# A gated cross-attention and quantised feed-forward layer on one core: VectorE's 128x4 passes take two tensors, batch 1 is loaded later, GpSimd quantises the last 128 tokens of each batch, and the orders of all engines are listed anew

## What is computed

```python
x = x + tanh(g_xattn) * attention(layernorm(x), ctx)          # 16 heads, 64 keys, biases on q, k, v, o
h = bit_linear(layernorm(x), w1)                              # 256 -> 1024
h = silu(depthwise_conv1d(h, conv_w) + conv_b)                # 3 taps along the 512 tokens
x = x + tanh(g_ffn) * bit_linear(h, w2)                       # 1024 -> 256
# bit_linear: act_quant rounds every token to 8 bits by its own largest |value|,
#   scale = 127 / clip(max|x|, 1e-5); weight_quant makes w -1, 0 or +1 by the mean |w|
```

## Time and profile before

| | |
|---|---|
| median of 3 runs | 168.42 us (167.06 to 169.79) |
| the profiled execution's own time | 169.36 us |
| its span, first to last instruction | 167.2 us |
| PE busy | 143.8 us (86%) |
| VectorE busy | 135.2 us (81%) |
| ScalarE busy | 112.3 us (67%) |
| GpSimd busy | 88.3 us (53%) |
| mean granted TensorE clock | 0.98 of full speed |

### The profile page before, as it was taken

One profiled execution on the slowest core, in us unless ns is written; L12 is line 12 of the kernel. 1 busy time (PEld: TensorE's weight loads), 2 busy tenths in 40 slices (PEclk: granted clock), 3 DMA queues, 4 the chain that ended last, 5 costly groups with the idle time before them and its releaser, 6 DMA issues.

```text
span 167.2 us, 3548 instructions
## 1 busy us (share of the span) xinstructions
PE 143.8 (86%) x1314; PEld 79.1 (47%) x1324; DVE 135.2 (81%) x240; ACT 112.3 (67%) x176; POOL 88.3 (53%) x88
## 2 busy tenths in 40 slices
PE   7839979999799999999999796999565999984792
PEld 3238435424565336652576242568333353743461
DVE  6455999961953669995837999999999969989993
ACT  0304598779616488899999997999498586652220
POOL 0204899999910542398370089882979943200330
PEclk9996999999999999999999999999998799999999
DMA  4999800000000000000000000000030000110024
GB/s 134 269 386 395 339 6 0 4 0 0 0 0 2 4 0 0 0 0 4 4 2 0 4 0 2 0 6 0 0 125 0 4 4 0 67 67 0 3 79 169
DMA packets 5919, 8.68 MB, mean 52 GB/s; under 512 B 528, under 2 KB 4880, under 8 KB 5648
## 3 DMA queue, kind: packets, MB, share of 16 engines
q1 hardware_dynamic: 4608, 5.51, 9.6%
q10 hardware_dynamic: 1296, 2.97, 4.7%
HBM read 6.38 MB, written 2.10 MB: 51 GB/s over the span
## 4 chain that ended last, share of the span: by engine, by line
PE 29%; DVE 24%; ACT 24%; issue 15%; DMA 5%; ACTq 1%; DVEq 0%
ACT hid L1181 6%; DMA w_attn<-attn_w 5%; PE ps L445 5%; DVE u L790 4%; DVE mx L720 4%; ACT probs L1120 3%; PE ps L311 3%; DVE hid_q L860 3%; DVE hmax L812 3%; PE ps L348 3%; PE ps L507 2%; ACT side L1169 2%; ACT xn L1079 2%; PE ps L397 2%; DVE top L768 2%
## 5 line engine op out<-in xcount | busy, mean ns | idle before, releaser
L790 DVE TENSOR_TENSOR u<-ps,deq_b 128x512 f32<-128x512 f32 x32 | 20.2, 679 | 4.1 <-PE ps L436 3.6
L1433 POOL TENSOR_TENSOR hid<-hid,side 128x512 f32<-128x512 f32 x12 | 15.6, 1305 | 8.8 <-ACT side L1166 8.8
L720 DVE TENSOR_REDUCE mx<-ps 128x16 f32<-128x1024 f32 x16 | 18.8, 1212 | 1.4 <-PE ps L321 1.4
L445 PE MATMUL ps<-u,conv_w 32*32 32x512 f32 (+1 forms) x576 | 18.5, 544 | 0.9 <-ACT hid L1188 0.7
L1120 ACT ACTIVATE probs<-ps 128x1024 f32<-128x1024 f32 x16 | 15.4, 1029 | 5.6 <-PE ps L348 5.5
L1445 POOL TENSOR_TENSOR x_s<-x_s,grown 128x512 f32<-128x512 f32 x6 | 7.6, 1277 | 21.1 <-ACT grown L1198 21.1
L860 DVE TENSOR_TENSOR hid_q<-hid,ps 128x1024 f16<-128x1024 f32 x16 | 18.6, 1215 | 0.0
L436 PE MATMUL ps<-xqT,w1q 128*128 128x512 bf16 x57 | 15.3, 397 | 3.6 <-ACT xqT L1139 2.9
L1440 POOL TENSOR_TENSOR hid<-hid,side 128x512 f32<-128x512 f32 x12 | 15.5, 1305 | 4.2 <-ACT side L1169 3.8
L507 PE MATMUL ps<-w2q,hid_q 128*128 128x256 f16 x128 | 15.6, 273 | 1.3 <-DVE hid_q L860 1.3
L311 PE MATMUL ps<-xT,w_attn 128*128 128x512 f32 x32 | 15.0, 601 | 0.9 <-DVE mx L720 0.9
(11 more groups left out here) (125 smaller groups left out, 307.2 us busy)
## 6 DMA issues: line engine op xcount, KB each, us to landing
x_s<-x SPq DMA_DIRECT2D x4, 512.0 KB, 12.2
out<-x_s SPq DMA_DIRECT2D x6, 256.0 KB, 2.1
hid<-w_t SPq DMA_DIRECT2D x1, 1024.0 KB, 18.4
hid<-w_t ACTq DMA_DIRECT2D x1, 1024.0 KB, 12.3
w_attn<-attn_w ACTq DMA_DIRECT2D x1, 512.0 KB, 10.0
out<-x_s SPq DMA_DIRECT2D x4, 128.0 KB, 1.8
conv_w<-conv_d ACTq DMA_DIRECT2D x1, 384.0 KB, 13.1
w_attn<-attn_w SPq DMA_DIRECT2D x1, 256.0 KB, 5.7
```

Of the source, the lines that this page charges most:

```text
L445: last = nc.tensor.matmul(ps[ROWS * g:ROWS * g + ROWS, banks[s], first:first + n], conv_w[rg, 4 * q + s, tap, :], u[rg, 4 * q + s, first + ...
L720: nc.vector.tensor_reduce(mx[:, b % 2, k, 0:HEADS], ps[:, bank:bank + 2, :].rearrange("p c (h k) -> p (c h) k", k=KEYS), AX.X, ALU.max).th ...
L790: nc.vector.tensor_tensor(u[:, f, 1:N + 1], ps[:, bank, :], deq1_b[:, b % 2, :], ALU.mult).then_inc(u_ready.sem, 1)
L1433: nc.gpsimd.tensor_tensor(dst, dst, side[:, m % TMPS, 0, :], ALU.add).then_inc(left_ready.sem, 1)
```

## The change

Five things are edited.

1. VectorE's small passes over one value for each token (128x4, or 128x2 for batch 3's halves) were TENSOR_SCALAR with constants. They become TENSOR_TENSOR or SCALAR_TENSOR_TENSOR, whose second operand is a constant kept in SBUF and repeated over the four columns. The pass that negates the mean is left out where ScalarE doesn't need it: of 8 such passes 3 stay (batch 1 of the first norm, batches 0 and 1 of the second). The norms subtract the mean instead.
2. SP waits for the k weights before it issues x of batches 1, 2, 3 and the second layer's weights.
3. The last tile of 128 tokens of each batch (k = 3) is quantised by GpSimd. GpSimd can't read the scale from PSUM there, so PE puts this block's scale in the next bank, ScalarE copies it to SBUF (`take_scale2`, 128x128, four times), and GpSimd multiplies.
4. VectorE sets four more constants at the start.
5. The lists of PE, VectorE, ScalarE and GpSimd are written anew, in other orders and with other PSUM banks.

```diff
+TURNED = frozenset([0, 1, 2, 3])
...
             sp.dma_start(w_attn[:, 0], attn_w[:, 0]).then_inc(wq_in, 16)
+            sp.wait_ge(wk_in, 16)
             sp.dma_start(x_s[:, 1], x_v[1]).then_inc(x_ins[1], 16)
...
-                nc.vector.tensor_scalar(var[:, b], mv[:, b, :, 1], LN_EPS, None, ALU.add).then_inc(var_ready.sem, 1)
-                nc.vector.tensor_scalar(minus_mean[:, b], mv[:, b, :, 0], -1.0, None,
-                                        ALU.mult).then_inc(var_ready.sem, 1)
+                nc.vector.tensor_tensor(var[:, b], mv[:, b, :, 1], eps[:].to_broadcast([P, T]),
+                                        ALU.add).then_inc(var_ready.sem, 1)
+                if b in SCALED:
+                    nc.vector.tensor_tensor(minus_mean[:, b], mv[:, b, :, 0], minus_one[:].to_broadcast([P, T]),
+                                            ALU.mult).then_inc(mean_ready.sem, 1)
...
-                nc.vector.tensor_scalar(step1[:, a], top1[:, a], CLIP, 1.0 / QMAX, ALU.max,
-                                        ALU.mult).then_inc(step1_ready.sem, 1)
+                nc.vector.scalar_tensor_tensor(out=step1[:, a], in0=top1[:, a], scalar=CLIP,
+                                               in1=step_of[:, 0:1].to_broadcast([P, T]), op0=ALU.max,
+                                               op1=ALU.mult).then_inc(step1_ready.sem, 1)
...
-                nc.vector.tensor_scalar(deq1[:, a], step1[:, a], wmean[:, 0:1], None,
+                nc.vector.tensor_tensor(deq1[:, a], step1[:, a], wmean[:, 0:1].to_broadcast([P, T]),
                                         ALU.mult).then_inc(scale1_ready.sem, 1)
...
+            def take_scale2(b, bank):
+                act.wait_ge(*(scale2_half_ps(0, 1) if b == SPLIT else scale2_ps(b)))
+                n = nth(b, TURNED)
+                if n:
+                    act.wait_ge(*hq_turned(n - 1))
+                nc.scalar.copy(scale2_col, ps[:, bank, (T - 1) * P:T * P]).then_inc(col_ready.sem, 1)
...
+            def quantise_hidden(b, k):
+                pool.wait_ge(*col_ready(nth(b, TURNED)))
+                if b:
+                    pool.wait_ge(*f2_ps(b - 1, k // 2))
+                tile = slice(k * P, (k + 1) * P)
+                nc.gpsimd.tensor_tensor(
+                    hid_q[:, :, tile].rearrange("p (q i) n -> p q i n", i=2),
+                    hid[:, b % 2, 0:FP, tile, :].rearrange("p q n i -> p q i n"),
+                    scale2_col.unsqueeze(1).unsqueeze(1).to_broadcast([P, FP, 2, P]),
+                    ALU.mult).then_inc(hq_turned.sem, 1)
...
             residual2(1, 0)
             residual2(1, 1)
+            quantise_hidden(2, 3)
             residual2(2, 0)
             residual2(2, 1)
+            quantise_hidden(3, 3)
```

More of the change, by code:

```diff
@@ L477, in spread_scale2_half @@
                 for k in (2 * a, 2 * a + 1):
-                    last = nc.tensor.transpose(ps[:, bank, k * P:(k + 1) * P],
+                    at = bank + (b in TURNED and k == T - 1)
+                    last = nc.tensor.transpose(ps[:, at, k * P:(k + 1) * P],
                                                qscale2[:, b % 2, k:k + 1].to_broadcast([P, P]), idf[:])
@@ new lines, in _ @@
+            hidden(0, 3, 7, p_ready(2, 0))
+            hidden(0, 4, 2, p_ready(2, 1))
+            hidden(0, 5, 3, p_ready(2, 1))
+            hidden(0, 6, 6, u_ready(0, 2))
+            hidden(0, 7, 7, u_ready(0, 3))
+            scores(3, 2, 4, p_ready(2, 2))
+            denominators(2, 0, 2, u_ready(0, 4))
+            values(2, 0, 3, u_ready(0, 5))
+            denominators(2, 1, 2)
+            values(2, 1, 0, p_ready(2, 3))
+            scores(3, 3, 6, u_ready(0, 7))
+            turn_den(2, 1, p_ready(2, 3))
@@ new lines, in _ @@
+            scores_t(3, 0, 6, deq1_ready(1), neg_ready(3))
+            scores_t(3, 1, 2, hid_ready(0, 3))
+            hidden(1, 2, 1, x1_ready(2, 0))
+            hidden(1, 3, 0, u_ready(1, 1))
+            scores_t(3, 2, 4, u_ready(1, 0), x1_ready(2, 1))
+            scores_t(3, 3, 6, p_ready(3, 0))
+            denominators(3, 0, 2, p_ready(3, 1))
+            values(3, 0, 3, p_ready(3, 1))
+            denominators(3, 1, 2)
+            values(3, 1, 1, u_ready(1, 2))
+            turn_hmax(0, 0, u_ready(1, 3))
@@ new lines, in _ @@
+            project_o(3, 0, 1, oT_ready(3, 0))
+            project_o(3, 1, 0, oT_ready(3, 1))
+            hidden(2, 0, 2, xqT_ready(2))
+            second(0, 0, 1, x1_ready(3, 0))
+            hidden(2, 1, 0, x1_ready(3, 1))
+            hidden(2, 2, 4, hid_taken(0, 2))
+            hidden(2, 3, 5, hid_ready(1, 0))
+            hidden(2, 4, 3, hid_ready(1, 1))
+            hidden(2, 5, 2, u_ready(2, 0))
+            hidden(2, 6, 0, u_ready(2, 1))
+            hidden(2, 7, 4, u_ready(2, 2))
+            second(0, 1, 5, u_ready(2, 3))
@@ new lines, in _ @@
+            convolve(2, 0, (0, 4, 6, 7), u_ready(2, 7), hid_ready(1, 3))
+            spread_deq1(3, 1, z_ready(0, 0))
+            turn_xq(3, 5, z_ready(0, 1))
+            hidden(3, 0, 5, xqT_ready(3))
+            turn_hmax(1, 3, u_ready(2, 4))
+            hidden(3, 1, 2, u_ready(2, 5))
+            hidden(3, 2, 0, hid_ready(2, 0))
+            hidden(3, 3, 1, deq1_ready(3))
+            hidden(3, 4, 5, u_ready(3, 0))
+            hidden(3, 5, 4, hid_ready(2, 1))
+            hidden(3, 6, 6, hid_ready(2, 2))
@@ L671, in _ @@
+            second(2, 0, 7, col_ready(2))
+            second(2, 1, 6, hid_taken(2, 2))
+            turn_hmax_half(3, 0, 7, z_ready(0, 4))
+            turn_hmax_half(3, 1, 4, hid_half(0, 2))
+            spread_scale2_half(3, 0, 5, hid_half(0, 3))
+            spread_scale2_half(3, 1, 2, hid_half(0, 6))
+            second(3, 0, 3, col_ready(3))
+            second(3, 1, 2, hid_taken(3, 2))
         @block.vector
```

681 lines of the change are left out of this document (324 added, 357 removed).

## The result

The changed kernel takes 176.92 us (median; 174.19 to 178.27) against 168.47 (167.06 to 169.79) for the kernel before on the same chip. The ratio is 1.042, with a 95% interval from 1.025 to 1.059: slower by 8.5 us by the medians, where 163.6 us was forecast and 159.2 to 168.0 given as the range.

A forecast was written before the change was run, and what follows sets the result against it. No engine bounds it throughout, but VectorE does from 97 to 156 us; terms -4.6 tiles, -0.4 passes left out, -1.0 start, +0.4 waits, +0.5 taps, +0.3 copies make -4.8: 163.6 us against 168.42, range 159.2 to 168.

The forecast's parts named there:

- the five passes: VectorE's mean-negating passes left out: worth between 0 and 0.85 us, taken as -0.4 us.
- The start: Loads up to the first row maximum: k weights at 8.5 us, first maximum near 22.7; -1.0 us, bounds -3.4 and +2.
- the start gives it back: Rival: x of batch 3 lands 2 us later, so the start's -1.0 becomes +2.0; 166.6 us, chance 0.17.
- The small passes: VectorE's 22 passes on six lines, 10.4 us with 6.7 of waits for GpSimd; waits taken to grow, +0.4 us.
- waits stay: The forecast's own case: small VectorE passes still wait for GpSimd; 163.6 us, range 161.5 to 166, chance 0.43.
- The tiles: Four quantiser tiles moved to GpSimd at 2.6 us each: -4.6 us on VectorE, +0.5 for taps, +0.3 for copies.
- a slow tile: Rival: GpSimd's tile takes longer than 2.6 us, delaying `second` on PE; 172.4 us at 5.2 per tile, chance 0.10.
- The lists: New instruction orders: 0 us, bounds -2 and +2, as VectorE idles only 3.2 us between 97 and 156 us.
- The clock: PE at half clock from 13 to 15 us; a shorter gap before it may save about 1 us.
- the tile and the end: Signs: GpSimd's tile at 2.4 to 2.6 us; VectorE's last three tiles in 3.5 us, GpSimd's done before them.
- The small lines: Sign on L702, L779, L794, L801, L854, L859: mean near 0.17 us says waits gone, 0.3 to 0.9 says they stay.
- The sign for the loads: The prediction would be wrong if x of batches 1 to 3 landed later than 19.5 us.

The follow-up runs named there:

- e13: Changed kernel with SP's wait out and scale2's small passes in PSUM, GpSimd's norms still subtracting: 170.97 us, ratio 1.015 to the kernel before.
- e4: Kernel before with only GpSimd's norms changed, to subtract the mean: 178.50 us, ratio 1.057.
- e12: Changed kernel with GpSimd's norms adding and scale2's small passes in PSUM, SP's wait kept where the change has it: 167.47 us, ratio 0.987 to the kernel before.
- e11: Kernel before with only SP's wait for the k weights added, ahead of x of batches 1 to 3: 169.47 us, ratio 1.008.
- e6: Changed kernel with GpSimd's norms adding, SP's wait out and scale2's small passes in PSUM: 162.79 us, ratio 0.960 to the kernel before.
- e3: Changed kernel with GpSimd's norms adding the negated mean and SP's wait out: 168.79 us, ratio 0.984 to the kernel before.
- e7: Changed kernel with norms adding, SP's wait out and all 16 last-layer quantiser tiles on VectorE: 171.53 us, ratio 1.005 to the kernel before.
- e8: Kernel before with GpSimd's norms reading the mean from `mv` but still adding it: 169.32 us in one execution.
- e14: e3 run again for a second trace: 168.69 us in one execution.
- e1: Changed kernel with only GpSimd's norms put back to adding the negated mean: 173.37 us, ratio 1.025 to the kernel before.
- e5: Changed kernel with norms adding, SP's wait out and VectorE's small passes in the old TENSOR_SCALAR form: 167.54 us, ratio 0.988 to the kernel before.

## Why the prediction was wrong

- **The step that failed first** is one that has no term in the sum. The description of the change says "The norms subtract the mean instead"; the prediction counts the five passes that this leaves out at 0.4 us and takes the norms themselves as unchanged. They cost GpSimd 13.4 us, more than its four tiles (9.7), and 8.2 to 9.4 us of time (e13, e4). No row of before could give the price of a subtraction on GpSimd; but an operation without a row wanted two bounds, as the two-tensor passes got, and none was written.
- **The start** was forecast as a gain of 1.0. The k weights landed near 9.06 us (8.5 forecast) and PE's first matmul on them came at 9.19: right. The rule for the rest looked only at the *last* load, x of batch 3. The one that decides is x of batch 1, because VectorE's list has its statistics ahead of the values and of everything else; it landed at 16.4 us. The prediction names what is queued behind the held SP, but of batch 1 it follows only ScalarE's norm, not VectorE's list. The rival "the start gives it back" had the right place, the first row maxima, and nearly their delay (2 us; 26.13 is 2.8 later), but it names the wrong load (VectorE comes to the statistics of batches 2 and 3 at 22.42 us and doesn't wait for them), and it has no idle PE and no clock in it. Measured, the wait costs +4.7 us in the new lists (e12) and +1.4 in the old (e11).
- **The small passes** were put down as "waits stay", and that is half of what happened. In single passes L702 took 2.20 us, L801 1.04, L859 1.12, L870 0.91, held by GpSimd to its end each time. But the 22 passes of the six lines took 7.7 us where they took 10.4; at 0.13 to 0.16 us for one that isn't held, some 4.4 us of that are waits, against 6.7 before: a third of the waits went, and the sum had them grow by 0.4. The Trainium skill (SBUF — State Buffer, "Who interferes with whom") says that a VectorE instruction with two SBUF inputs contends with a GpSimd instruction that reads SBUF; the trace agrees, with 2.20 us for 0.16 of work. Its other half, that a VectorE instruction with at most one SBUF input and outside the two-port modes doesn't contend with GpSimd, agrees with e6's 0.17 us. How long such a pass waits isn't GpSimd's busy share, by which the prediction scaled it: beside the same run of additions it was 4.85 us in e3 and 1.09 in e7.
- **The tiles** were right in their durations: GpSimd's took 2.43 us (2.6 forecast; 2.37 to 5.2 given), ScalarE's copy 0.27 (0.3), VectorE's last three 3.48 (3.45). The rival of a slow tile didn't occur. Of their worth in time, 3.4 us in the sum (4.6 less 0.5, 0.3 and 0.4), no run shows it alone: e7's 2.7 to 3.5 us are near it, with a difference in the waits beside them.
- **The lists** were taken at 0 with bounds of 2 us. e3 and e6 differ by 4.0 to 6.0 us, in e3's trace most of it through one wait in one place of the new order, so these bounds were too narrow: an order's worth isn't limited by the idle time in VectorE's row, since a held pass counts as busy. In the changed kernel this wait was short (0.24 and 1.12 us), so it is no part of the miss.
- **The clock** was read only at 13 to 15 us. Each of the large losses came with a second one there: a gap on PE, and then work at 1.2 GHz or near it (6.44 us for 3.67 us of q projection, 5.11 for 3.40 of convolution).

Of the listed signs, the tile and the end held. The small lines gave no single answer: means of 0.67 (L702), 0.46 (L859) and 0.36 us (L801) told "stay", 0.16 (L794), 0.19 (L854) and 0.23 (L779) told "gone" or nearly so. The sign for the loads, x of batches 1 to 3 later than 19.5 us, would have passed the load that did the harm (16.4 us), and there was no sign for the norms. With the two faults out and the waits of `scale2` taken away, the kernel comes to 162.8 us, 0.8 below the forecast; that is not the forecast's case, which had the waits in it. Put into the prediction's own sum, the two failed steps give the miss to within 0.6 us: 163.6 + 8.2 (subtraction, e13) + 5.7 (start, +4.7 by e12 for -1.0) = 177.5 us, and 176.92 was measured. The other terms can still be off against one another.

## What to carry to other kernels

Price every line that a diff rewrites, also one that seems to compute the same with another sign: an operation that the trace has never shown on that engine gets two bounds. For a load that is held back, follow the list of each engine that waits for it up to the next thing that PE needs; the first late load matters, not the last. A small VectorE pass that reads SBUF beside a busy GpSimd should be priced between one GpSimd instruction and the longest unbroken run of them near it (1.09 and 4.85 us here); with its operands in PSUM it took 0.17 to 0.19 us here (e6), which is worth trying wherever such a pass stands ahead of PE. And faults undone one at a time can hide each other: build up from the mended kernel as well.

## What was not expected of the hardware

- GpSimd's 128x256 float32 pass with two values for each row takes 1.22 us when its first operation subtracts and 0.55 us when it adds (e4, e8); VectorE's takes the same time either way.
- A VectorE pass with two SBUF tensors was not let in between four GpSimd instructions that followed one another: 4.85 us in e3 and 4.84 in e14 and e1. In e7 the same pass at the same place was let in after one (1.09 us), as was the one-tensor form (1.06 us, e5).
- Not every GpSimd instruction holds such a pass: at 25.94 us in the changed kernel one took 0.16 us while GpSimd's 128x4 powers ran from 25.69 to 27.67 us.
- One gap of 4.01 us on PE (e3) was followed by a clock of 0.52, and the convolution behind it took 1.7 us longer: two fifths of the gap again.
